# Two attention stages of a fused transformer kernel: heads normalised four at a time over DRAM, and row maxima seeded by their plain half

## The chip, the cores and the metric

The kernel runs on one core of one Trainium2 chip. The time is the device time of one execution in microseconds, the median of several runs. The names in the profile are PE for TensorE's matmuls, PEld for its weight loads, DVE for VectorE, ACT for ScalarE, POOL for GpSimd, and SP (SPq) for the queue of SyncE, which issues the DMAs spoken of here.

## The reference

Input x is 2 x 1024 tokens of 512 features in float32. Six blocks are added to it in turn, each on the layer norm of x:

```
x = x + 0.5 * ffn0(ln(x))          stage 0, f0: quantised, hidden 1536
x = x + attn0(ln(x))               stage 1, a0: 16 query heads, 4 kv heads, rope, biases
x = x + 0.5 * ffn0(ln(x))          stage 2, f0
x = x + 0.5 * ffn1(ln(x))          stage 3, f1: hidden 2048
x = x + attn1(ln(x))               stage 4, a1: 16 heads
x = x + 0.5 * ffn1(ln(x))          stage 5, f1

attention of one head, head size 32, 1024 tokens:
  att = q @ k.T / sqrt(32), causal mask, softmax over keys
  y   = att @ v ;  out = concat(heads) @ Wo
```

## The kernel before

One program, `make_plan`, writes a list of steps in order. Each engine walks that list and issues its own part of each step, so the list fixes the order on every engine and on the queue of SP. Semaphores carry the dependences. PSUM has eight banks, and `bank_turns` assigns them along the plan with a rough pace model (`Pace`).

An attention stage (stages 1 and 4) has two batches of 16 heads, 32 heads in all, in eight **groups** of four (numbered 0 to 7; `HPG` is 4). A head has eight **units** of 128 keys, a group has 32 units. Unit `u` of the main loop in `attention` issues, in this order: the side jobs that are due (`side.tick`), the row maxima of unit `u + 13` (`row_unit`, `AHEAD` is 13), the scores of the unit's keys against all later queries (`key`, L1148, whose exponential ScalarE takes at L1335), the diagonal mask and sum of two units on GpSimd (`e_mask` L1660, `e_add` L1671), and at odd units the products with v and with ones for two units nine back (`pv` L1167, `den` L1178). Beside the loop run side jobs: the projection of the next group (`piece`, L1094), layer norms, the output projection.

**Row maxima.** For a tile of 128 queries `row` (L1130) makes the scores against all earlier keys. Up to 512 keys are one piece, more are two equal halves (`row_pieces`). VectorE takes the minimum of the negated masked scores of each piece with `tensor_tensor_reduce` (L1501), which also writes into PSUM and is followed by a read of the accumulator. Second halves go to columns 8 to 11 of `negmax`, and `row_min` (L1510) joins them. The eight maxima are transposed (`m_tp`, L1137), split in two (`m_hi`, `m_lo`) and written by SP into two rows of the query stack (`m_lo`, L1755), which `key` waits for.

**Stacks.** Before the rows of a group can run, SP copies each head's projected q (in stage 4, and every fourth group of stage 1, k as well) into `qst` and `kst`, three DMAs each (`stack`, L1745). The four heads of the next group are stacked at units 18, 20, 26 and 31 (`STACKS_AT`). Since rows run 13 units ahead, the first row of the next group stands in unit 19.

**The end of a head.** `pv` and `den` leave in one bank 256 columns of sums and 256 columns of denominators, in four quarters of 32 partitions, the same denominator in all 32 partitions of a quarter. `y_fin` takes the reciprocal of 128x256 (L1540) and multiplies (L1544) into `ysb`, and frees the bank; `y_move` (L1764) brings the four quarters into the head's 32 partitions of `y`. After the fourth head of a group `y_hi` (ScalarE, L1343) and `y_lo` (VectorE, L1554) make `yT`, and eight output products (`oproj`) and additions (`x_sum`, L1568) follow, one a unit, at units 16 to 23 of the next group. `y` is one tile: `y_move` waits for `y_lo` of the group before.

```
for c in range(HPG):
    sp.dma_start(T[s]["y"][j * HD:(j + 1) * HD, c * QUAD:(c + 1) * QUAD],
                 T[s]["ysb"][n % 2][c * HD:(c + 1) * HD, :]).then_inc(moved[n % 2], 16)
```

Of the kernel before, what the change touches and what calls it, by code (L numbers as in the profile page):

```python
# [8 lines left out]
F32 = mybir.dt.float32  # L9
# [8 lines left out]
P = 128  # L18
# [36 lines left out]
YT_AT = 2  # L55
O_LAG = 1
# [27 lines left out]
def into_heads(s):  # L84
    return s + 1 < len(STAGES) and not is_ffn(s + 1)

# [50 lines left out]
def make_plan():  # L137
# [112 lines left out]
    def attention(s, left):  # L250
# [18 lines left out]
        def row_unit(u):  # L269
            n, i = divmod(u, ST)  # L270
            if n < HEADS_ALL:
# [3 lines left out]
                if i == ST - 1:  # L275
                    plan.append(("row_min", s, n))
# [45 lines left out]
        for g in range(GROUPS_ALL):  # L322
# [6 lines left out]
            put([split(s, "o", g, 0)], at + O_W_AT, 0)  # L329
# [18 lines left out]
        def times_v(n, jt):  # L348
# [5 lines left out]
            if k == PAIRS - 1:  # L354
                job = [[]] * Y_AT + [[("y_fin", s, n)]] + [[]] * Y_WAIT + [[("y_move", s, n)]]
                g, j = divmod(n, HPG)
                if j == HPG - 1:
                    job += [[]] * YT_AT + [[("y_hi", s, g)]] + [[("y_lo", s, g)]] + [[]] * O_LAG
                    job += timed(*((O_STEP * t, ("oproj", s, g, t)) for t in range(ST)),
                                 *((O_STEP * t + X_AFTER, ("x_sum", s, g, t)) for t in range(ST)))  # L360
                side.start(job)
# [63 lines left out]
    "row": ("s_q", "row_max"), "row_min": ("row_min",), "m_tp": ("m_tp",), "m_hi": ("m_hi",), "m_lo": ("m_lo",),  # L425
    "key": ("s_k", "exp"), "e_mask": ("e_mask",), "pv": ("pv",),
    "e_add": ("e_add",), "den": ("den",), "y_fin": ("y_rec", "y_fin"),
# [59 lines left out]
class Pace:  # L487
# [10 lines left out]
    def run(self, step, banks):  # L498
# [84 lines left out]
        elif kind == "y_fin":  # L583
            done[step] = work("dve", 0.9, ("pv", s, where[0], ST - 1))
        elif kind == "y_hi":
            done[step] = work("act", 1.1, ("y_fin", s, (where[0] + 1) * HPG - 1))
# [9 lines left out]
def bank_turns(plan):  # L596
# [5 lines left out]
    for step in plan:  # L602
        width = banks_wanted(step)
        needs = []
        if width:
# [13 lines left out]
            if step[0] == "pv":  # L619
                release["y_fin", step[1], step[2]] = mine  # L620
# [44 lines left out]
def build(nc, a, out):  # L665
# [6 lines left out]
    with ExitStack() as ctx:  # L672
# [17 lines left out]
        moved = [ctx.enter_context(nc.semaphore(f"moved{i}")) for i in range(2)]  # L690
        stored = ctx.enter_context(nc.semaphore("stored"))
# [26 lines left out]
        for s, kind in enumerate(STAGES):  # L718
            t = T[s] = {}
            with ExitStack() as sc:  # L720
# [47 lines left out]
                else:  # L768
# [12 lines left out]
                    t["negmax"] = [sbuf(sc, f"{tag}negmax{i}", [P, ST + CT]) for i in range(2)]  # L781
# [7 lines left out]
                    t["rden"] = [sbuf(sc, f"{tag}rden{i}", [P, QUAD]) for i in range(2)]  # L789
                    t["ysb"] = [sbuf(sc, f"{tag}ysb{i}", [P, QUAD]) for i in range(2)]  # L790

        def gave_way(s):
# [123 lines left out]

        def quarters_of(y):
# [931 lines left out]
```

## Time and profile before

| | |
|---|---|
| Runs | 2629.57, 2633.96, 2639.21 us, median 2633.96 |
| Span of the profiled execution | 2632.3 us (the profile gives no other time of its own for it; it lies between the runs) |
| PE busy, PEld busy | 2535.4 us (96%), 2013.0 us (76%) |
| DVE, ACT, POOL busy | 1533.2 (58%), 1035.6 (39%), 981.6 us (37%) |
| First attention stage, units of groups 0 to 7 | 344 to 763 us of the span |
| Second attention stage, the same | 1623 to 2076 us |
| DMA traffic | 128.73 MB, mean 49 GB/s |

Busy shares of the whole span mix stages with different limits. The two attention stages take a third of the time, and only they are touched. The two feed-forward kinds run matmul after matmul. In the attention stages all four compute engines and SP take part, and what sets the time must be read from who waits for whom there. Matmuls are pipelined and their ends are modelled, so a busy PE is not PE at its peak.

### The profile page before, as it was taken

To read this page: it belongs to the slowest core of one execution; us is meant where nothing else is said; L and a number is where in the kernel's file an instruction comes from. 1 tells how busy PE (TensorE), PEld (TensorE's weight loads), DVE (VectorE), ACT (ScalarE), POOL (GpSimd) and SP (SyncE) were. 2 spreads that over 40 slices of the span, in tenths; PEclk is the share of its full clock that TensorE was granted. 3 is DMA by queue.
4 is the path that set the end of the run, shared out by engine and by line. 5 is a ranking of instruction groups with operands and counts; after the bars stand their busy time and mean duration, and the time that the engine had idled before them with its cause. 6 is when DMAs were issued, how large, how long until landed. Compare 5 with 4: busy or idle time off the path is not lost.

```text
span 2632.3 us, 44135 instructions
## 1 busy us (share of the span) xinstructions
PE 2535.4 (96%) x16928; PEld 2013.0 (76%) x16928; DVE 1533.2 (58%) x3356; ACT 1035.6 (39%) x1885; POOL 981.6 (37%) x1373
## 2 busy tenths in 40 slices
PE   6999989999999999999999999999999999999999
PEld 4788867667668888888888878677776678888887
DVE  7777579979975445433333345798589643333333
ACT  6555346656653223311111133566466431111111
POOL 5333566666643225211111122666366521111110
PEclk9999989999999999999999999999999999999999
DMA  4222131222220110100000002343233100000001
GB/s 148 73 73 73 39 76 46 51 68 64 48 93 1 36 45 12 37 25 25 24 25 25 25 17 58 92 94 75 52 88 79 37 32 25 24 25 25 25 17 64
DMA packets 72002, 128.73 MB, mean 49 GB/s; under 512 B 15728, under 2 KB 24944, under 8 KB 71792
## 3 DMA queue, kind: packets, MB, share of 16 engines
q1 hardware_dynamic: 71792, 125.92, 17.3%
q8 instruction: 134, 2.20, 0.4%
q14 instruction: 76, 0.62, 0.1%
HBM read 62.42 MB, written 13.63 MB: 29 GB/s over the span
## 4 chain that ended last, share of the span: by engine, by line
PE 81%; DVE 6%; POOL 2%; ACT 2%; SPq 2%; issue 2%; DMA 1%; DVEq 0%; ACTq 0%; POOLq 0%
PE psum L1049 65%; PE psum L1167 5%; PE psum L1130 4%; PE psum L1148 4%; PE psum L1178 2%; DVE psum L1501 2%; SPq L1745 1%; PE psum L1058 1%; DVE s1a0rden L1540 1%; ACT s1a0e L1335 1%; SPq L1764 0%; POOL s1a0e L1671 0%; ACT s4a1e L1335 0%; PE psum L1137 0%; POOL rstd L1610 0%
## 5 line engine op out<-in xcount | busy, mean ns | idle before, releaser
L1501 DVE CUSTOM_DVE_ANT_0 psum<-psum,mask_q 128x512 f32<-128x512 f32 (+5 forms) x768 | 413.2, 574 | 101.2 <-PE psum L1130 97.3
L1049 PE MATMUL psum<-hA_hi,wmem 128*128 128x256 f32 (+1 forms) x1536 | 405.2, 334 | 0.5 <-DVE s1a0negmax L1501 0.3
L1049 PEld LDWEIGHTS psum<-hA_hi,wmem 128*128 128x128 f32 x1536 | 270.3, 190 | 31.8 <-DVE s1a0negmax L1501 1.5
L1049 PE MATMUL psum<-hA_lo,wmem 128*128 128x512 f32 (+1 forms) x864 | 293.8, 340 | 0.0
L1335 ACT ACTIVATE s4a1e<-psum,p_scale 128x384 f32<-128x384 f32 (+5 forms) x384 | 205.5, 581 | 95.2 <-PE psum L1148 91.8
L1335 ACT ACTIVATE s1a0e<-psum,p_scale 128x384 f32<-128x384 f32 (+5 forms) x384 | 202.4, 578 | 78.1 <-PE psum L1148 76.8
L1454 DVE SCALAR_TENSOR_TENSOR x<-psum,x 128x512 f32<-128x512 f32 x256 | 175.7, 689 | 97.4 <-PE psum L1049 93.9
L1425 DVE TENSOR_TENSOR s5f1prod<-psum,s5f1silu 128x512 f32<-128x512 f32 x64 | 44.2, 691 | 303.7 <-PE psum L1049 303.7
L1425 DVE TENSOR_TENSOR s3f1prod<-psum,s3f1silu 128x512 f32<-128x512 f32 x64 | 44.2, 691 | 294.2 <-PE psum L1049 294.2
L1635 POOL TENSOR_TENSOR wmem<-raw,wmem 128x512 fp32r<-128x512 f32 x58 | 74.3, 1290 | 315.7 <-ACT wmem L1237 315.7
L1049 PE MATMUL psum<-s3f1w,s3f1a 128*128 128x512 f32 x768 | 181.6, 390 | 0.9 <-POOL s3f1w L1635 0.9
L1049 PE MATMUL psum<-s5f1w,s5f1a 128*128 128x512 f32 x768 | 180.0, 390 | 1.6 <-POOL s5f1w L1635 1.6
L1049 PEld LDWEIGHTS psum<-hA_lo,wmem 128*128 128x128 f32 x864 | 164.8, 191 | 19.8
L1671 POOL TENSOR_TENSOR s4a1e<-s4a1e 128x896 f32<-128x896 f32 (+3 forms) x128 | 164.8, 1288 | 17.4 <-ACT s4a1e L1335 6.4
L1671 POOL TENSOR_TENSOR s1a0e<-s1a0e 128x896 f32<-128x896 f32 (+3 forms) x128 | 164.6, 1286 | 17.1 <-ACT s1a0e L1335 5.8
L1049 PEld LDWEIGHTS psum<-s5f1w,s5f1a 128*128 128x128 f32 x768 | 143.9, 188 | 32.3 <-issue 2.0
L1049 PEld LDWEIGHTS psum<-s3f1w,s3f1a 128*128 128x128 f32 x768 | 143.5, 188 | 31.1 <-DVE s3f1prod L1425 1.1
L1645 POOL TENSOR_TENSOR x<-x,s0f0dso 128x512 f32<-128x512 f32 x64 | 89.0, 1412 | 136.1 <-DVE s0f0dso L1449 136.1
L1660 POOL TENSOR_SCALAR_AFFINE_SELECT s4a1e<-s4a1e 128x128 f32<-128x128 f32 x256 | 74.9, 299 | 166.6 <-ACT s4a1e L1335 164.9
L1635 POOL TENSOR_TENSOR s5f1w<-raw,s5f1w 128x512 fp32r<-128x512 f32 x32 | 40.8, 1296 | 242.4 <-ACT s5f1w L1237 242.4
L1635 POOL TENSOR_TENSOR s3f1w<-raw,s3f1w 128x512 fp32r<-128x512 f32 x32 | 40.8, 1295 | 241.4 <-ACT s3f1w L1237 241.4
L1148 PE MATMUL psum<-s1a0qst,s1a0kst 98*128 98x384 f32 (+4 forms) x384 | 118.1, 362 | 12.9 <-ACT s1a0e L1335 7.8
(195 smaller groups left out, 5581.8 us busy)
## 6 DMA issues: line engine op xcount, KB each, us to landing
s1a0qst<-s1a0qs SPq DMA_DIRECT2D x96, 128.0 KB, 2.3
s4a1qst<-s4a1qs SPq DMA_DIRECT2D x96, 128.0 KB, 2.4
s4a1kst<-s4a1ks SPq DMA_DIRECT2D x96, 128.0 KB, 2.4
raw<-in_gate SPq DMA_DIRECT2D x44, 256.0 KB, 2.9
raw<-in_up SPq DMA_DIRECT2D x44, 256.0 KB, 2.8
raw<-in_down SPq DMA_DIRECT2D x44, 256.0 KB, 2.8
rounded<-s0f0w SPq DMA_DIRECT2D x24, 256.0 KB, 2.0
s2f0w<-rounded SPq DMA_DIRECT2D x24, 256.0 KB, 4.9
```

The costliest lines, as they stand in the source:

```text
L1049: ins = pe.matmul(out_, w, m, start=n == 0, stop=n == len(terms) - 1)
L1130: pe.matmul(ps[:, 0, 0:pw], q_st[0:STACK, j, i * P:(i + 1) * P], k_st[0:STACK, j, z * pw:(z + 1) * pw], start=True, stop=True).then_inc(se ...
L1148: pe.matmul(ps[:, 0, 0:pw], k_st[0:STACK + 2, j, jt * P:(jt + 1) * P], q_st[0:STACK + 2, j, q0 + z * pw:q0 + (z + 1) * pw], start=True, st ...
L1167: ins = pe.matmul(psum[c * HD:(c + 1) * HD, bank, jt * HD:QUAD], v[:, jt, kv, :], e[:, :, c, :], start=jt == 0, stop=jt == ST - 1, skip_gr ...
L1335: act.activation(T[s]["e32"][:, begin_ + z * pw:begin_ + (z + 1) * pw - skip], src, ACT.Exp, bias=p_scale[:]).then_inc(sem["exp"], 1)
L1425: dve.tensor_tensor(prod[:], psum[:, bank, :], silu[:], ALU.mult).then_inc(sem["prod"], 1)
L1454: dve.scalar_tensor_tensor(x[:, tile, :], src, 0.5, x[:, tile, :], ALU.mult, ALU.add).then_inc(sem["x_add"], 1)
L1501: dve.tensor_tensor_reduce(scores, scores, mask_q[:, first:first + pw], -1.0, -MASKED, ALU.add, ALU.min, T[s]["negmax"][n % 2][:, column:c ...
L1635: pool.tensor_tensor(lo, buf[:], hi.bitcast(F32), ALU.subtract).then_inc(sem["w_lo"], 1)
L1645: pool.tensor_tensor(x[:, tile, :], x[:, tile, :], T[s]["dso"][nth(*step) % 2][:], ALU.add).then_inc(sem["x_pool"], 1)
L1660: pool.affine_select(out=block, in_=block, compare_op=ALU.is_ge, fill=0.0, base=0, pattern=[[1, P]], channel_multiplier=-1).then_inc(sem[" ...
L1671: pool.tensor_tensor(e32[:, begin + P:end], e32[:, begin + P:end], e32[:, more:more_end], ALU.add).then_inc(sem["e_add"], 1)
```

## The change

For groups 0 to 6 of each stage (`in_place(g)` is true for group 7 alone) the end of a head goes another way:

- `y_out`: ScalarE copies the whole bank, 128x512, to `ysb` (now 512 columns wide), where the plan had `y_fin`.
- `y_save`: SP writes `ysb` to DRAM (`heads_out`, 256 KB). After the fourth head, `y_load` reads the sums of each head back into its 32 partitions of `y` (four DMAs of 128 KB a group), and `den_in` reads one denominator of each query into a compact tile of 128x32 (16 KB).
- `y_rec`: VectorE takes the reciprocal of that tile. `y_keep` writes it to DRAM (`rdens`), `y_spread` reads it back with each head's row repeated over its 32 partitions (128x1024, 512 KB) into `yT[HI]`, which is free then. `y_norm`: VectorE multiplies `y` by it, 128x1024.
- `y_hi`, `y_lo` and the output products follow, nine units later than before: `y_lo` stands at unit 23 and the products at units 25 to 32. The output weight of the next group is fetched after the products, not at unit 23.

Group 7 keeps `y_fin` and `y_move`. The plan places of one group are, counted in units of the group after it: `y_out` of its last head 7, `y_save` 9, last `y_load` and `den_in` 12, `y_rec` 14, `y_keep` 15, `y_spread` 17, `y_norm` 21, `y_hi` 22, `y_lo` 23.

Row maxima in two pieces: the first half, which has no masked element, is now a `tensor_reduce` with maximum and negation straight from PSUM; the second half's `tensor_tensor_reduce` takes that result as its initial value and waits for its semaphore. `row_min` and the four extra columns are gone. `Pace` gets new durations for these steps, which moves bank assignments.

```
-                plan.append(("row_min", s, n))
...
                 g, j = divmod(n, HPG)
+                if in_place(g):
+                    job = [[]] * Y_AT + [[("y_fin", s, n)]] + [[]] * Y_WAIT + [[("y_move", s, n)]]
+                    job += [[]] * YT_AT
+                else:
+                    job = [[]] * Y_AT + [[("y_out", s, n)]] + [[]] * SAVE_WAIT
+                    job += [[("y_load", s, m) for m in range(n - j, n) if j == HPG - 1]
+                            + [("y_save", s, n)]]
+                    job += [[]] * LOAD_WAIT
                 if j == HPG - 1:
+                    if not in_place(g):
+                        job += timed((0, ("y_load", s, n)), (0, ("den_in", s, g)),
+                                     (REC_AT, ("y_rec", s, g)), (KEEP_AT, ("y_keep", s, g)),
+                                     (SPREAD_AT, ("y_spread", s, g)), (NORM_AT, ("y_norm", s, g)))
+                    job += [[("y_hi", s, g)]] + [[("y_lo", s, g)]] + [[]] * O_LAG
...
+                negmax = T[s]["negmax"][n % 2][:, i:i + 1]
+                if z + 1 < row_pieces(i):
+                    dve.tensor_reduce(negmax, scores, AX.X, ALU.max,
+                                      negate=True).then_inc(sem["row_max"], 1)
+                    return
+                if z:
+                    on.wait_ge(sem["row_max"], at("row_max", "row", s, n, i, z - 1))
+                dve.tensor_tensor_reduce(scores, scores, mask_q[:, first:first + pw], -1.0,
+                                         negmax if z else -MASKED, ALU.add, ALU.min,
+                                         negmax).then_inc(sem["row_max"], 1)
...
+            def y_out(s, n):
+                if n >= 2:
+                    on.wait_ge(*ysb_left(s, n - 2))
+                on.wait_ge(sem["pv"], at("pv", "pv", s, n, ST - 1))
+                act.activation(T[s]["ysb"][n % 2][:], psum[:, banks["pv", s, n, 0][0], :],
+                               ACT.Copy).then_inc(sem["y_out"], 1)
...
+            def y_rec(s, g):
+                on.wait_ge(den_loaded, 16 * (nth("y_rec", s, g) + 1))
+                dve.reciprocal(T[s]["rden"][:], T[s]["den"][:]).then_inc(sem["y_rec"], 1)
+
+            def y_norm(s, g):
+                on.wait_ge(y_loaded, HPG * 16 * (nth("y_norm", s, g) + 1))
+                on.wait_ge(rden_spread, 16 * (nth("y_norm", s, g) + 1))
+                y = T[s]["y"]
+                dve.tensor_tensor(y[:], y[:], T[s]["spread"], ALU.mult).then_inc(sem["y_norm"], 1)
...
+            def y_keep(s, g):
+                k = nth("y_keep", s, g)
+                on.wait_ge(sem["y_rec"], at("y_rec", "y_rec", s, g))
...
+            def y_spread(s, g):
+                k = nth("y_spread", s, g)
+                on.wait_ge(rden_kept, 16 * (k + 1))
+                if g:
+                    on.wait_ge(sem["o_proj"], at("o_proj", "oproj", s, g - 1, ST - 1))
+                sp.dma_start(T[s]["spread"], rdens[k % 2].unsqueeze(1).broadcast_to([HPG, HD, SEQ])
+                             ).then_inc(rden_spread, 16)
```

How the instructions move, in three places. First VectorE in units 14 and 15 of group 5 in the first stage, before (`ISA` is the maximum and the accumulator read behind it, in turn):

```order
L1501 ISA psum,s1a0negmax<-psum,mask_q 128x448
L1501 ISA s1a0negmax 128x1
L1501 ISA psum,s1a0negmax<-psum,mask_q 128x448
L1501 ISA s1a0negmax 128x1
L1554 TENSOR_TENSOR s1a0yT<-s1a0y,s1a0yT 128x1024
L1501 ISA psum,s1a0negmax<-psum,mask_q 128x512
L1501 ISA s1a0negmax 128x1
L1501 ISA psum,s1a0negmax<-psum,mask_q 128x512
L1501 ISA s1a0negmax 128x1
L1540 RECIPROCAL s1a0rden<-psum 128x256
L1544 TENSOR_TENSOR s1a0ysb<-psum,s1a0rden 128x256
```

and in the changed kernel:

```order
L1563 TENSOR_REDUCE s1a0negmax<-psum 128x1
L1568 ISA psum,s1a0negmax<-psum,mask_q,s1a0negmax 128x448
L1568 ISA s1a0negmax 128x1
L1607 RECIPROCAL s1a0den<-s1a0den 128x32
L1563 TENSOR_REDUCE s1a0negmax<-psum 128x1
L1568 ISA psum,s1a0negmax<-psum,mask_q,s1a0negmax 128x512
L1568 ISA s1a0negmax 128x1
```

The plain half is one instruction in place of two. `y_rec` (the 128x32 reciprocal) stands between rows 6 and 7, where `y_lo` stood; the wide reciprocal and product of the head are gone.

Second the queue of SP in the same group, units 12 to 20, before (`s1a0mrow` is `m_lo`, `raw<-in_q` a weight, `s1a0qst<-s1a0qs` a stack, `s1a0y<-s1a0ysb` is `y_move`):

```order
L1764 DMA s1a0y<-s1a0ysb 32x256 x4
L1755 DMA s1a0qst<-s1a0mrow 1x8x128 x2
L1723 DMA raw<-in_q 128x512
L1745 DMA s1a0qst<-s1a0qs 32x1024 x3
L1764 DMA s1a0y<-s1a0ysb 32x256 x4
L1745 DMA s1a0qst<-s1a0qs 32x1024 x3
L1755 DMA s1a0qst<-s1a0mrow 1x8x128 x2
```

and in the changed kernel (`rdens<-s1a0den` is `y_keep`, `s1a0yT<-rdens` `y_spread`, `heads_out<-s1a0ysb` `y_save`):

```order
L1856 DMA s1a0den<-heads_out 128x1x32
L1821 DMA s1a0qst<-s1a0mrow 1x8x128 x2
L1864 DMA rdens<-s1a0den 128x32
L1789 DMA raw<-in_q 128x512
L1872 DMA s1a0yT<-rdens 128x1x1024
L1839 DMA heads_out<-s1a0ysb 128x512
L1811 DMA s1a0qst<-s1a0qs 32x1024 x6
L1821 DMA s1a0qst<-s1a0mrow 1x8x128 x2
```

`y_keep`, `y_spread` and the save of the next group's first head now stand ahead of the first stack; before, `y_move` of that head stood behind it.

Third SP at the end of group 7, from unit 12 on, before:

```order
L1745 DMA s1a0qst<-s1a0qs 32x1024 x3
L1734 DMA wmem<-rounded 128x512
L1764 DMA s1a0y<-s1a0ysb 32x256 x4
L1755 DMA s1a0qst<-s1a0mrow 1x8x128 x2
L1734 DMA wmem<-rounded 128x512 x2
L1764 DMA s1a0y<-s1a0ysb 32x256 x4
```

and in the changed kernel:

```order
L1821 DMA s1a0qst<-s1a0mrow 1x8x128 x2
L1800 DMA wmem<-rounded 128x512
L1864 DMA rdens<-s1a0den 128x32
L1872 DMA s1a0yT<-rdens 128x1x1024
L1800 DMA wmem<-rounded 128x512
L1830 DMA s1a0y<-s1a0ysb 32x256 x4
L1821 DMA s1a0qst<-s1a0mrow 1x8x128 x2
```

The first `y_move` of group 7 stands ahead of the last `m_lo` in both; the `y_lo` of group 6 for which it waits has moved on VectorE from unit 14 to unit 23.

## Rows read from the trace of the kernel before

**Rows 1.** Stretches: us, busy (x) of PE, PEld, DVE, ACT, POOL, clock, DMA share, GB/s

```profile
616.00:664.00 48.00, 46.85 (x544) 34.60 (x547) 45.09 (x128) 29.50 (x59) 32.73 (x50) 1.00 0.24 57
...
1020.00:1600.00 580.00, 576.68 (x2611) 475.31 (x2610) 215.93 (x346) 141.88 (x240) 108.08 (x131) 1.00 0.09 26
```

**Rows 2.** Who waited (us, times) for L1501, L1335 and L1745, in turn

```profile
  PEld psum L1130: 8.7, 21
...
  PE psum L1049: 0.3, 2
...
  PEld psum L1148: 30.7, 44
...
  PE psum L1130: 5.4, 9
...
  PE psum L1130: 8.3, 6
```

**Rows 3.** Groups of instructions by line: busy us, mean ns, idle before

```profile
L1540 DVE RECIPROCAL s1a0rden<-psum 128x256 f32<-128x256 f32 x32 | 55.9, 1745 | 6.4 <-PE psum L1167 6.4
...
L1544 DVE TENSOR_TENSOR s1a0ysb<-psum,s1a0rden 128x256 f32<-128x256 f32 x32 | 13.6, 424 | 2.2
...
L1510 DVE TENSOR_TENSOR s1a0negmax<-s1a0negmax 128x4 f32<-128x4 f32 x32 | 14.9, 465 | 1.1
...
L1554 DVE TENSOR_TENSOR s1a0yT<-s1a0y,s1a0yT 128x1024 fp32r<-128x1024 f32 x8 | 9.9, 1234 | 1.6 <-ACT s1a0yT L1343 1.6
...
L1343 ACT ACTIVATE s1a0yT<-s1a0y 128x1024 fp32r<-128x1024 f32 x7 | 7.4, 1057 | 2.1 <-DMA s1a0y<-s1a0ysb 2.1
...
L1501 DVE CUSTOM_DVE_ANT_0 psum<-psum,mask_q 128x512 f32<-128x512 f32 x82 | 55.8, 707 | 18.2 <-PE psum L1130 18.2
```

**Rows 4.** Timeline of DVE, group 5, stage 1: start us, us, what

```profile
639.52 0.13 DVE L1501 DVE_READ_ACCUMULATOR2_ANT s1a0negmax<- 128x1 f32 x1
```

**Rows 5.** Timeline of SP and PE, the same group

```profile
638.17 0.43 SPq L1723 DMA_DIRECT2D raw<-in_q  x1
638.70 1.82 SPq L1745 DMA_DIRECT2D s1a0qst<-s1a0qs  x3
...
639.80 0.63 PE L1148 MATMUL psum<-s1a0qst,s1a0kst 98*128 98x512 f32 x2
...
640.83 0.47 PE L1049 MATMUL psum<-s1a0ow,s1a0yT 128*128 128x512 f32 x1 [0.40 <-issue]
...
644.94 0.86 PE L1049 MATMUL psum<-s1a0ow,s1a0yT 128*128 128x512 f32 x3
645.64 0.40 PE L1130 MATMUL psum<-s1a0kst,s1a0qst 96*128 96x512 f32 x1
```

**Rows 6.** DMA issues: queue, op, count, KB each, median us to landing

```profile
s1a0qst<-s1a0qs SPq DMA_DIRECT2D x96, 128.0 KB, 2.3
...
rounded<-s0f0w SPq DMA_DIRECT2D x24, 256.0 KB, 2.0
```

**Rows 7.** Timeline of PE, group 5 of stage 4

```profile
1950.14 0.62 PE L1148 MATMUL psum<-s4a1qst,s4a1kst 98*128 98x512 f32 x2
...
1955.38 0.39 PE L1130 MATMUL psum<-s4a1kst,s4a1qst 96*128 96x512 f32 x1
```

**Rows 8.** Timelines of ACT, SP and PE at the end of stage 1

```profile
754.98 0.47 ACT L1335 ACTIVATE s1a0e<-psum,p_scale 128x256 f32<-128x256 f32 x1 [1.17 <-PE psum L1148]
...
748.06 2.48 SPq L1764 DMA_DIRECT2D s1a0y<-s1a0ysb  x4
...
752.48 1.38 SPq L1755 DMA_DIRECT2D s1a0qst<-s1a0mrow  x2
...
756.91 1.04 PE L1148 MATMUL psum<-s1a0qst,s1a0kst 98*128 98x512 f32 x4
```

**Rows 9.** Stretches around a wait for a stack; columns as in rows 1

```profile
534.00:537.00 3.00, 1.11 (x6) 0.62 (x4) 2.76 (x4) 1.54 (x4) 2.84 (x3) 1.00 0.61 132
537.00:541.00 4.00, 3.46 (x28) 2.08 (x29) 1.30 (x3) 0.95 (x2) 2.31 (x4) 0.57 0.33 76
```

More of the change, by code:

```diff
@@ L328, in attention @@
                 put(group_weights(s, g + 2), at + QK_W_AT, 2)
-            put([split(s, "o", g, 0)], at + O_W_AT, 0)
+            if g == 0:
+                put([split(s, "o", g, 0)], at + O_W_AT, 0)
             if g % HPG == 2:
@@ L424 @@
     "bias_x": ("x_pool",),
-    "row": ("s_q", "row_max"), "row_min": ("row_min",), "m_tp": ("m_tp",), "m_hi": ("m_hi",), "m_lo": ("m_lo",),
+    "row": ("s_q", "row_max"), "m_tp": ("m_tp",), "m_hi": ("m_hi",), "m_lo": ("m_lo",),
     "key": ("s_k", "exp"), "e_mask": ("e_mask",), "pv": ("pv",),
-    "e_add": ("e_add",), "den": ("den",), "y_fin": ("y_rec", "y_fin"),
+    "e_add": ("e_add",), "den": ("den",), "y_fin": ("y_den", "y_fin"), "y_out": ("y_out",),
+    "y_rec": ("y_rec",), "y_norm": ("y_norm",),
     "y_hi": ("y_hi",), "y_lo": ("y_lo",), "oproj": ("o_proj",), "x_sum": ("x_add",),
@@ L690, in build @@
         moved = [ctx.enter_context(nc.semaphore(f"moved{i}")) for i in range(2)]
+        saved = [ctx.enter_context(nc.semaphore(f"saved{i}")) for i in range(2)]
+        y_loaded = ctx.enter_context(nc.semaphore("y_loaded"))
+        den_loaded = ctx.enter_context(nc.semaphore("den_loaded"))
+        rden_kept = ctx.enter_context(nc.semaphore("rden_kept"))
+        rden_spread = ctx.enter_context(nc.semaphore("rden_spread"))
+        heads_out = nc.dram_tensor("heads_out", (2, HPG, P, CH), F32, kind="Internal").ap()
+        rdens = nc.dram_tensor("rdens", (2, HPG, SEQ), F32, kind="Internal").ap()
         stored = ctx.enter_context(nc.semaphore("stored"))
@@ L915, in y_moved, with y_saved, ysb_left, y_whole @@
             return moved[n % 2], HPG * 16 * (nth("y_move", s, n) // 2 + 1)
+        def y_saved(s, n):
+            return saved[n % 2], 16 * (nth("y_save", s, n) // 2 + 1)
+        def ysb_left(s, n):
+            return y_moved(s, n) if in_place(n // HPG) else y_saved(s, n)
+        def y_whole(s, g):
+            if in_place(g):
+                return [y_moved(s, n) for n in range((g + 1) * HPG - 2, (g + 1) * HPG)]
+            return [(sem["y_norm"], at("y_norm", "y_norm", s, g))]
         def quarters_of(y):
@@ L1572, in vector_program @@
                      "q8": q8_, "q_b": q_b, "gu": gu, "a_lo": a_lo, "down": down,
-                     "turned": turned, "row": row, "row_min": row_min, "m_lo": m_lo, "v_out": v_out,
-                     "y_fin": y_fin, "y_lo": y_lo, "x_sum": x_sum, "piece_lo": piece_lo}
+                     "turned": turned, "row": row, "m_lo": m_lo, "v_out": v_out,
+                     "y_fin": y_fin, "y_rec": y_rec, "y_norm": y_norm, "y_lo": y_lo, "x_sum": x_sum, "piece_lo": piece_lo}
             for kind, *where in plan:
@@ L1769, in sync_program @@
+            steps = {"begin": begin, "open": open_, "y_move": y_move, "y_save": y_save, "y_load": y_load, "den_in": den_in,
+                     "y_keep": y_keep, "y_spread": y_spread, "x_in": x_in_, "w_in": w_in, "w_keep": w_keep,
                      "w_back": w_back, "stack": stack, "m_lo": m_lo}
```

99 lines of the change are left out of this document (63 added, 36 removed).

## The prediction

> **What bounds the kernel now.** I read the stretches first, one line for each group of four heads. A group without layer-norm work takes 48.0 us in the first attention stage: VectorE is busy for 45.1 of them, 94%, and TensorE for 46.9, 98%, so both look full [rows 1]. The waits tell them apart [rows 2]. In the whole span TensorE (matmuls and weight loads together) waited 20.9 us for the row maxima of L1501, in eight rows of which the first and the last are shown. For the exponentials of ScalarE, L1335, it waited four times as long: six rows from 30.7 to 5.4 us, 86 us together. Nobody waited for the reciprocal L1540. So VectorE is nearly full and yet seldom what TensorE waits for: it runs a unit or two behind TensorE and catches up inside the group. That limits the gain from a lighter VectorE to about 21 us of direct waits, of which I take 20, and a share of the 86 us that can't be read off.
>
> **What VectorE is spared, per group of four heads.** Removed: four reciprocals of 1.745 us and four products of 0.424 us, 8.7 us, and four row_min of 0.465 us, 1.9 us [rows 3]. Added: one reciprocal of 128x32, an eighth of the elements of L1540, so 0.2 us plus a fixed part, 0.3 us; one 128x1024 product like L1554, 1.2 us [rows 3]. The 16 unmasked halves lose the accumulator read of 0.13 us [rows 4], 2.1 us, and each masked half now waits for the semaphore of its plain half and reads a seed. No row shows a PSUM tensor_reduce. The nearest is L1501 itself, 0.707 us at 512 columns [rows 3]. If the reduce takes as long, 2.1 us are saved less 16 waits of 0.05 to 0.1 us; I take 1 us, with ends of 0 and 3. Sum: 8.7 + 1.9 + 1 - 0.3 - 1.2 = 10 us of 45. The Trainium skill, "VectorE: DVE Perf Modes", Rules for kernel authors, speaks against this part: tensor_reduce on a hot path is called the slowest DVE op, better restructured. By that rule the spared time would be 9 us and not 10, which changes no bound here.
>
> **What goes to ScalarE.** Four copies of 128x512 from PSUM per group. ScalarE is busy for 29.5 of 48 us [rows 1], so there is room, but each copy stands just before the two widest exponentials of the next head. The split of the output weight, which stood at unit 24 and ahead of the same exponentials, moves to a lighter place, and the bank of a head's output is free sooner. I cost these together at 0, with -10 and +15 us as ends.
>
> **The stack behind the new waits, a moved step that costs.** This is what the sum turns on. SP is one queue in order. At unit 14 or 15 it now meets y_keep, which waits for y_rec; then y_spread, which waits until y_keep has landed in DRAM; then the save of the next group's first head; and only then, at unit 18, the stack of that same next group's first head. TensorE needs that stack in unit 19, because rows run 13 units ahead of keys. Before, the stack had only finished pieces ahead of it and went out early. In group 5 of the first stage its three DMAs are issued from 638.70, its row matmul runs at 645.64, nearly 7 us later [rows 5].
>
> Now the same place after the change. The last maximum of row 6 ends at 639.65 [rows 4], so y_rec ends near 639.9. y_keep goes out at 639.95 and lands after 2.0 us, the time of a write to DRAM [rows 6]: 641.95. y_spread and y_save take about 0.45 us each to issue, as the whole-tile load ahead of the stack does (0.43) [rows 5]: 642.9. The three stack DMAs are issued in 1.82 us [rows 5], the third starts at 644.1 and lands 2.3 us later [rows 6]: 646.4. When is it wanted? From the key of unit 16 (639.80) to the row of unit 19 (645.64) are 5.84 us [rows 5]. They hold three output tiles of 0.70 us (644.94 to 645.64) and a wait of 0.4 us in front of them (640.83); these tiles move to units 25 on. That leaves 3.3 us, so it is wanted at 643.1. **TensorE waits 3.3 to 3.4 us.** In the second stage k is stacked too. Unit 16's key is at 1950.14 and the row at 1955.38 [rows 7]; less three tiles, 1953.3. The units ahead of it hold twice the projections, so VectorE is earlier against TensorE there; I put y_rec at 1949.2. Then 2.0 for y_keep, 0.9 for two issues, 3.0 until the sixth stack DMA starts, 2.3 to land: 1957.5. Wait 4.2 us. There are six groups per stage with both a spread and a following stack: 6 x 3.4 + 6 x 4.2 = 46 us. Waits for stacks cost 8.3 us now [rows 2] and are in that number already: **+38 us**. Ends: +15 if the chain is 2 us shorter than I think each time; +60 if the 512 KB spread and the 256 KB save, which stand in the DMA queue right ahead of the stack, hold up its landing by 1.5 us more.
>
> The Trainium skill, "DMA: Bandwidth & Descriptors", section "Latency and other measured facts", gives 0.8 us as the shortest round trip to DRAM, for tiny transfers such as this one of 16 KB. By that figure y_keep would cost 1.2 us less each time and the sum 14 us less. No row here shows so small a write, and the 2.0 us of the trace stand.
>
> **The last group.** It is normalised in place, and its first y_move waits for y_lo of group 6, since both use the one y tile. y_lo moves from unit 14 to unit 23; y_move stays at unit 18. SP stands still, and behind it is m_lo of head 31, which the key of unit 24 needs. Timed on the first stage [rows 8]: the exponential of unit 22 ends at 755.45, y_hi adds 1.06, y_lo 1.22 [rows 3], four y_move 2.48, the second m_lo starts 0.7 later and lands after 2.0 at most: 762.9. The key now starts at 756.91, and two output tiles ahead of it are gone. Wait 6 to 7.4 us per stage: **+14 us**, ends 6 and 20.
>
> **The clock.** From 534 to 537 TensorE was busy for 1.1 us only, since it waited for a stack; in most of the next 4 us the granted clock was at its lower level, 1.2 GHz [rows 9]. A mean of 0.57 over 4 us loses 1.7 us. I have 14 waits of 3.3 us or more and take it for five: **+8 us**, ends 0 and 24.
>
> **The sum.** 2632.3 (span) - 20 + 0 + 38 + 14 + 8 = 2672. The span of the profiled execution is 1.7 us under the median of the three runs (2634.0), so I take 2672 as the time too: 1.4% slower. A measurement of this kernel can tell about 0.3%, 8 us.
>
> **Rivals.**
> - *VectorE sets the pace (faster).* For: 94% busy against 72% for weight loads in the same line, 34.6 of 48 us, while the long feed-forward stretch reaches 82%, 475 of 580 us [rows 1]. By the Trainium skill, "Perfetto Trace Analysis", Identifying the Most-Contended Engine, matmul busy time doesn't count and the engine of highest occupancy is the one to relieve, which would be VectorE. Worked from the rows: the direct 21 us and a third of the 86 us go, 50 us, while SP's chain turns out shorter (+15) and the last group costs 10: 2607. Half of the 86 us and no stall at all would be 2568. Against: who waits for whom. Chance 0.18.
> - *It cancels.* The relief of the rival above with the stalls I forecast, less the clock: -50 + 38 + 14 = +2, 2634. Chance 0.10.
> - *The stalls as forecast, and the clock drops at nearly each of them, with transfers colliding:* -20 + 60 + 14 + 22 = +76, 2708. Chance 0.2, a part of slower.
> - *The maxima change nothing* (reduce, semaphore and seed eat the accumulator read and row_min): VectorE is still 7 us lighter per group; the time moves by under 5 us within the cases above.
>
> **How the numbers follow.** Slower, as forecast or worse: 0.52 + 0.2 = 0.72. Within 0.3%: 0.10. Faster: 0.18. The range leaves out the better half of the fast rival and what lies beyond the clock case: 2608 to 2712. Within the slower cases it is 2645 to 2712.
>
> **What would show it.** Right: in groups 1 to 6 TensorE waits for a DMA on the stacks at its row matmul (L1130 before), 3 us or more each, and group 5 of the first stage takes 49 us or more although VectorE's busy time in it falls to some 35 us; on SP the first stack of a group is issued after, not before, unit 17; near the end of both stages one wait of 6 us for the DMA of mrow; clock rows at 0.5 behind such waits. A reciprocal of about 0.3 us and a norm of 1.2 us. Wrong: groups of 45 us or less, stacks that land in time, or y_rec much earlier against TensorE than I timed it. If waits for the exponentials of ScalarE fall by more than a third, my bound on the gain was wrong.

## The result and the profile after

The changed kernel takes 2822.01 us (median of 4 runs, 2819.5 to 2827.24) against 2636.59 us before in the same session: a ratio of 1.071, 95% interval 1.0689 to 1.0732. The forecast was 2672, 1.4% slower; it is 7.1% slower, and the range ended at 2712.

The page of the changed kernel (line numbers are now the changed kernel's: rows L1184, keys L1202, stack L1811, y_keep L1864, y_spread L1872, y_save L1839):

```profile
span 2820.2 us, 43813 instructions
...
PE 2578.7 (91%) x16928; PEld 2042.8 (72%) x16928; DVE 1430.7 (51%) x2952; ACT 1060.1 (38%) x1941; POOL 990.3 (35%) x1373
...
PEclk9999998998989999999999999988988899999999
```

The span grew by 187.9 us. VectorE's busy time fell by 102 us; the forecast's 10 us in each of 14 groups would have made it 140. TensorE fell from 96 to 91% busy. The view of waits says what TensorE stood for (us in total, times, longest):

```profile
PE psum L1184 <- DMA s4a1kst<-s4a1ks: 78.9, 7, 14.0
PE psum L1184 <- DMA s1a0qst<-s1a0qs: 53.5, 5, 12.0
...
PE psum L1202 <- DMA s1a0qst<-s1a0mrow: 14.0, 4, 11.1
PE psum L1184 <- DMA s1a0kst<-s1a0ks: 13.9, 2, 11.7
...
PE psum L1202 <- DMA s4a1qst<-s4a1mrow: 10.1, 3, 8.1
```

The three rows on L1184 are the waits for stacks, 146.3 us in 14 waits, against 8.3 us before [rows 2]. Two of the 14 are short and have no spread in front of them: 2.1 us at the start of the first stage (2.1 before as well) and 3.3 us in group 0 of the second. The other twelve stand one in each of groups 1 to 6 of both stages, as forecast: 10.0 to 12.0 us each in the first stage and 11.9 to 14.0 in the second, 140.9 us together, where the forecast had 3.4 and 4.2. The two rows on L1202 hold the wait for m_lo at the end of each stage, 11.1 and 8.1 us, also where the forecast put it. One of the waits for a stack, in group 1 of the first stage, in the timelines of SP and then of PE:

```profile
412.35 0.35 SPq L1864 DMA_DIRECT2D rdens<-s1a0den  x1
412.74 0.44 SPq L1789 DMA_DIRECT2D raw<-in_q  x1
413.80 0.59 SPq L1872 DMA_DIRECT2D s1a0yT<-rdens  x1
414.45 0.46 SPq L1839 DMA_DIRECT2D heads_out<-s1a0ysb  x1
415.02 3.76 SPq L1811 DMA_DIRECT2D s1a0qst<-s1a0qs  x6
```

```profile
414.47 0.51 PE L1202 MATMUL psum<-s1a0qst,s1a0kst 98*128 98x384 f32 x2
425.32 0.77 PE L1184 MATMUL psum<-s1a0kst,s1a0qst 96*128 96x512 f32 x1 [10.35 <-DMA s1a0qst<-s1a0qs]
```

On SP all goes as forecast: y_keep to the start of the stack's third DMA takes 3.9 us (the forecast had 4.1). Then the chain of waits shows what was not forecast: 8.91 us from that issue to its landing, where the forecast put 2.3.

```profile
415.64 0.59 SPq L1811
416.23 0.04 issue
416.27 8.91 DMA s1a0qst<-s1a0qs
```

The same time in stretches (columns as in rows 1):

```profile
413.00:417.00 4.00, 1.97 (x27) 1.00 (x19) 2.07 (x8) 2.70 (x6) 2.95 (x4) 1.00 0.66 184
417.00:421.00 4.00, 0.00 (x0) 0.00 (x0) 0.00 (x0) 0.24 (x1) 1.00 (x2) 0.57 0.85 181
421.00:425.00 4.00, 0.00 (x0) 0.00 (x0) 0.00 (x0) 0.00 (x0) 0.00 (x0) 0.50 0.25 94
425.00:429.00 4.00, 3.68 (x30) 2.30 (x31) 0.76 (x2) 0.95 (x3) 1.81 (x2) 0.50 0.01 5
660.51:725.06 64.55, 50.85 (x559) 36.88 (x558) 38.59 (x104) 31.34 (x63) 33.35 (x51) 0.87 0.26 67
```

The last row is group 5 of the first stage: 64.6 us, where it took 48.5 by the same cut (first key of one group to first key of the next), with VectorE busy for 38.6 of them.

The groups by that cut (group 7 to the last key of its stage), which the experiments are read against, in us:

| kernel | stage 1, groups 0 to 7 | stage 4, groups 0 to 7 |
|---|---|---|
| before | 48.0 48.5 56.7 61.2 58.1 48.5 56.8 41.5 | 50.3 53.8 60.3 56.7 77.2 53.0 59.0 43.1 |
| after | 42.5 60.3 69.8 70.1 72.3 64.5 69.5 51.2 | 49.9 67.2 75.6 70.9 92.3 71.1 74.4 56.4 |

Group 0 has no spread in it, and it became shorter, by 5.5 us in the first stage and 0.4 in the second. Every other one became 9 to 18 us longer.

### The profile page after: what moved, and what is told of

Read it like the earlier page. It is cut to its first block, busy times and chain, and to the rows that moved or that the text cites. A ratio compares the mean times of both kernels' runs of the same rounds, so it can differ in the third digit from the quotient of the medians.

```text
span 2820.2 us, 43813 instructions
## 1 busy us (share of the span) xinstructions
PE 2578.7 (91%) x16928; PEld 2042.8 (72%) x16928; DVE 1430.7 (51%) x2952; ACT 1060.1 (38%) x1941; POOL 990.3 (35%) x1373
## 4 chain that ended last, share of the span: by engine, by line
PE 77%; DMA 7%; DVE 6%; SPq 2%; issue 2%; ACT 2%; POOL 1%; DVEq 0%; ACTq 0%; POOLq 0%
PE psum L1103 62%; PE psum L1221 5%; PE psum L1184 4%; PE psum L1202 4%; DMA s4a1kst<-s4a1ks 2%; PE psum L1232 2%; DMA s1a0qst<-s1a0qs 2%; SPq L1811 1%; DVE psum L1568 1%; PE psum L1112 1%; DVE s1a0negmax L1563 1%; DVE s4a1negmax L1563 1%; DMA s1a0kst<-s1a0ks 0%; DMA rdens<-s4a1den 0%; PE psum L1191 0%
## 5 line engine op out<-in xcount | busy, mean ns | idle before, releaser
L1568 DVE CUSTOM_DVE_ANT_0 psum<-psum,mask_q 128x512 f32<-128x512 f32 (+3 forms) x256 | 125.4, 503 | 252.3 <-PE psum L1184 250.9
L1184 PE MATMUL psum<-s4a1kst,s4a1qst 96*128 96x512 f32 (+4 forms) x384 | 127.9, 392 | 80.6 <-DMA s4a1kst<-s4a1ks 78.9
L1486 DVE TENSOR_TENSOR s5f1prod<-psum,s5f1silu 128x512 f32<-128x512 f32 x64 | 44.3, 692 | 303.5 <-PE psum L1103 303.5
L1486 DVE TENSOR_TENSOR s3f1prod<-psum,s3f1silu 128x512 f32<-128x512 f32 x64 | 44.3, 692 | 294.1 <-PE psum L1103 294.1
L1184 PE MATMUL psum<-s1a0kst,s1a0qst 96*128 96x512 f32 (+4 forms) x384 | 127.1, 391 | 68.8 <-DMA s1a0qst<-s1a0qs 53.5
L1184 PEld LDWEIGHTS psum<-s4a1kst,s4a1qst 96*128 96x128 f32 x384 | 69.5, 200 | 103.4 <-issue 87.0
L1202 PE MATMUL psum<-s1a0qst,s1a0kst 98*128 98x384 f32 (+4 forms) x384 | 122.8, 372 | 22.7 <-DMA s1a0qst<-s1a0mrow 14.0
```

The costliest lines, as they stand in the source:

```text
L1184: pe.matmul(ps[:, 0, 0:pw], q_st[0:STACK, j, i * P:(i + 1) * P], k_st[0:STACK, j, z * pw:(z + 1) * pw], start=True, stop=True).then_inc(se ...
L1202: pe.matmul(ps[:, 0, 0:pw], k_st[0:STACK + 2, j, jt * P:(jt + 1) * P], q_st[0:STACK + 2, j, q0 + z * pw:q0 + (z + 1) * pw], start=True, st ...
L1486: dve.tensor_tensor(prod[:], psum[:, bank, :], silu[:], ALU.mult).then_inc(sem["prod"], 1)
L1568: dve.tensor_tensor_reduce(scores, scores, mask_q[:, first:first + pw], -1.0, negmax if z else -MASKED, ALU.add, ALU.min, negmax).then_inc ...
```

## The experiments

Three questions: what made the stacks land 9 us late; what the parts cost one by one; and what the idea could bring with all waits mended. The kernel before was timed beside every experiment, at a median of 2635.96 to 2638.67 us.

### The spread's transfer: same rows, or four heads outermost

`y_spread` is one DMA that reads four rows of 4 KB, each 32 times, as [4 heads, 32, 1024]. Theory S: the cut over the DMA engines goes by that outermost 4. Theory H: 128 reads of the same few rows hinder each other. First, other rows, same shape:

```
-sp.dma_start(T[s]["spread"], rdens[k % 2].unsqueeze(1).broadcast_to([HPG, HD, SEQ]))
+rows = heads_out[g % 2].rearrange("j (a b) q -> j a (b q)", b=2)[:, 0:HD, :]
+sp.dma_start(T[s]["spread"], rows)
```

> The changed kernel with y_spread reading 128 different rows of 4 KB (from heads_out, 4 heads x 32 rows) in place of each head's one row 32 times over; outermost dimension 4 as in the change. The normalisation then multiplies by other numbers: the spread of the reciprocals is left out, its transfer's size and shape are kept. Theory S: nothing changes, 2822 within 12, waits for stacks of 10 us each. Theory H: the transfer takes 3 us, waits of 2 to 5 us, 2690.

Measured: 2833.35 us, 1.0734 of before (1.0712 to 1.0756), against 1.071 for the change. The waits for stacks are 86.8, 60.2 and 15.9 us, 163 together. Reading 128 different rows is no faster, 11 us slower if anything: H falls, and the time lies within theory S's 12 us.

Then the same rows in another shape, one transfer for each head:

```
+for j in range(HPG):
+    sp.dma_start(T[s]["spread"][j * HD:(j + 1) * HD, :],
+                 rdens[k % 2, j].unsqueeze(0).broadcast_to([HD, SEQ]))
```

> The changed kernel with y_spread as four transfers, one for each head: 32 rows of 4 KB from that head's one row of DRAM, so that the outermost dimension of each is 32 and not 4; same place on SP, three more issues of 0.45 us ahead of the stack. Theory S (the one transfer of the change is cut along its outermost dimension of 4, so four of the sixteen DMA engines carry all of it and the stack's pieces queue behind it there): the four transfers use all sixteen, the spread is through in 2 to 3 us, and TensorE's 14 waits for stacks fall from 10.4 us each (146 us together) to 4 to 5 (the 3.4 of SP's queue and 1.3 for the issues), 65 us together; time 2715 (2695 to 2745). Theory Q (it is SP's order alone that makes the stack late): waits as before or longer, 2820 or more.

Measured: 2743.17 us, 1.0391 (1.0365 to 1.0416): 79 us less than the change, with the same 512 KB in four issues. Waits of TensorE, and the stretches that answer to those above:

```profile
PE psum L1184 <- DMA s4a1kst<-s4a1ks: 39.0, 7, 7.0
PE psum L1184 <- DMA s1a0qst<-s1a0qs: 29.6, 6, 5.8
```

```profile
415.50:419.50 4.00, 1.99 (x27) 0.99 (x19) 2.07 (x8) 2.65 (x6) 2.95 (x4) 1.00 0.66 196
419.50:423.50 4.00, 0.44 (x1) 0.47 (x2) 0.00 (x0) 0.30 (x1) 1.01 (x2) 0.79 0.96 246
423.50:427.50 4.00, 4.00 (x32) 2.50 (x32) 1.25 (x3) 1.21 (x3) 1.83 (x2) 0.50 0.11 24
```

The stretch at a share of 0.25 is gone: 0.96, then done. The waits are 75.1 us in 15 (with 6.5 in 2 for k). The twelve behind a spread take 67.3 of them, 5.3 us each in the first stage and 5.9 in the second. The forecast's 3.4 and 4.2 with three more issues of 0.45 would be 4.8 and 5.6. Together the two runs show that the way the transfer was cut made the landing late, not the rows read. The four transfers differ from the one in two things, the outermost dimension and the size of each; one transfer with the 32 rows outermost (`spread_turned`) gave no result, so these two aren't separated. That four engines carried it is read from the share of 0.25; which engine a packet ran on the profile doesn't show. The Trainium skill has this as a rule, "DMA: Bandwidth & Descriptors", Rules for kernel authors: an outermost dimension of fewer than 16, a leading zero-stride broadcast for example, confines the whole transfer to at most that many engines. Both runs agree with it: a share of 0.25 with 4 outermost, 0.96 with 32.

### The order on SP

Here the transfer stays as it is, and what waits moves behind the stacks; the edit of `tail_later` below is in it, with 12 units and not 6.

```
-REC_AT, KEEP_AT, SPREAD_AT, NORM_AT = 2, 3, 5, 9
+REC_AT, KEEP_AT, SPREAD_AT, NORM_AT = 2, 7, 9, 15
```

> The changed kernel with y_spread's transfer as it is (outermost dimension 4) but y_keep, y_spread and y_norm 4 to 6 units later, behind the first two stacks on SP, and the first y_move of the last group behind m_lo of head 31 (alone worth 16.5 us: 2805.5). The stacks have 7 units from issue to use where they stood 1. Theory: both, a late issue and the slow transfer ahead, hurt only because the stack is behind them; here the waits for stacks fall under 20 us together, the clock comes back, and the time is 2625 (2605 to 2650), whatever the spread takes. Rival: DMA engines are what is short: m_lo and the other stacks meet the spread instead, waits move to L1202 and to y_norm, 2680 or more.

Measured: 2753.27 us, 1.0426 (1.04 to 1.0452): 52 us less than `tail_later`, not 180. The time is the rival's, and so is half of its mechanism. The waits for stacks fell to 33 us (24.2, 4.7, 4.4) and those for m_lo are 5.8 us, but the slow transfer is now late for `y_norm`, on VectorE, and TensorE's row matmul waits for VectorE's row maxima:

```profile
DVE s4a1y L1615 <- DMA s4a1yT<-rdens: 32.0, 7, 7.6
...
DVE s1a0y L1615 <- DMA s1a0yT<-rdens: 20.7, 6, 6.0
...
PE psum L1186 <- DVE s4a1negmax L1565: 15.4, 5, 5.9
...
PE psum L1186 <- DVE s1a0negmax L1565: 12.2, 6, 2.8
```

VectorE stood for it 52.7 us with the row maxima queued behind. The slow transfer costs in both places that were tried. Both mended, `y_spread` as four transfers and `NORM_AT` 13:

> As order_tail, with y_spread as four transfers over all engines, and y_norm two units earlier. If the place in the queue is all that matters, within 8 us of order_tail. If the four loaded DMA engines still delay something (m_lo, later stacks), 10 to 30 us faster than order_tail. Against the kernel before: VectorE has 7 us less per group from the normalisation and 1.6 us more from the maxima; if VectorE sets the pace in the groups, 2570 to 2600; if TensorE does, 2610 to 2630.

Measured: 2697.67 us, 1.0224 (1.019 to 1.0258), 56 us less than with the slow transfer, more than the 10 to 30 expected if four loaded engines still delayed something (`y_norm` moved too). Still 60 us over before. The next section has its twin with the old maxima; SP's timeline there showed what was left in front of the stack:

```profile
1996.88 0.34 SPq L1844 DMA_DIRECT2D heads_out<-s4a1ysb  x1
1997.33 1.82 SPq L1816 DMA_DIRECT2D s4a1qst<-s4a1qs  x3
1999.19 1.85 SPq L1816 DMA_DIRECT2D s4a1kst<-s4a1ks  x3
```

The stack is issued 0.45 us after y_save (the row on heads_out), which waits for ScalarE's copy y_out; it starts 33.6 us after the start of its group. In the kernel before it started at 1947.22, 26.0 us after, and 2.9 before the key of unit 16 [rows 7]:

```profile
1947.22 2.63 SPq L1745 DMA_DIRECT2D s4a1qst<-s4a1qs  x3
```

The last groups were longer too, 47.6 and 49.4 us against 41.5 and 43.1. So y_save of a group's first head went behind the stack as well, and the delay by four units was dropped for group 6, which has no stack behind it:

```
+by = LATER if g + 2 < GROUPS_ALL else 0          # LATER = 4
-job = [[]] * Y_AT + [[("y_out", s, n)]] + [[]] * SAVE_WAIT
+job = [[]] * Y_AT + [[("y_out", s, n)]] + [[]] * (SAVE_WAIT + (2 if j == 0 else 0))
```

> The changed kernel with y_spread as four transfers, the first y_move of the last group behind m_lo of head 31, and SP's order mended wholly: y_keep, y_spread and y_norm four units later (but not in the group ahead of the last, which has no stack behind it), and the save of a group's first head behind the first stack and no longer ahead of it. Theory: in four_order_tail the stack still stood behind y_save, which waits for ScalarE's copy y_out (a stack issued at 1997.33, 0.45 behind the save), and the last groups lost 5 us each and 11 us at the end of the first stage to output tiles pushed behind the last head. With both mended the waits for stacks go back to the 8 us of the kernel before, and the time falls from 2698 to 2640 (2620 to 2660). Rival: ScalarE's copies and the larger traffic hold the time, 2675 or more.

Measured: 2661.12 us, 1.0083 (1.0065 to 1.0101), 1 us above the theory's range; waits for k stacks 11.8 and 4.7 us. The mean clock was 0.992 in the profiled execution, the fastest of six (2649.70), and 0.984 to 0.988 in the others; before it was 0.988 to 0.994. So the spread's shape, the places on SP and what followed from them (the clock among it) account for about 160 of the 185 us.

### The end of a stage

```
+wait = Y_WAIT + (MOVE_LATER if j == 0 else 0)     # MOVE_LATER = 6
-job = [[]] * Y_AT + [[("y_fin", s, n)]] + [[]] * Y_WAIT + [[("y_move", s, n)]]
+job = [[]] * Y_AT + [[("y_fin", s, n)]] + [[]] * wait + [[("y_move", s, n)]]
```

> The changed kernel with the first y_move of a head group that is normalised in place (head 28) six units later, behind m_lo of head 31. Theory: the waits of TensorE for m_lo at the end of the two stages, 11.1 and 8.1 us, were SP standing at that y_move for y_lo of group 6; they go, the last groups take 9 and 11 us less with the clock, 2802 (2795 to 2808). Rival: head 30's y_fin or the exponentials take the wait's place, under 8 us gained, 2814 or more.

Measured: 2805.53 us, 1.0637 (1.0621 to 1.0653): 16.5 us less than the change. Group 7 takes 45.8 and 44.3 us (51.2 and 56.4). In the first stage half of the wait is still there, 5.6 us of 11.1. The slow spread fits it: y_spread of group 6 was issued at 818.80 and m_lo of head 31 from 823.03, and from 826 to 830, with TensorE idle, the DMA share was 0.35. In `save_after_stack`, with four transfers, the waits for m_lo are 4.7 us in all. The forecast term was 14, and its mechanism holds.

### The maxima

The kernel before with the change's maxima alone (its diff is the part on `row` and `row_min` of the change):

> The kernel before with the maxima of the change alone: plain tensor_reduce on unmasked halves, their result as the masked half's initial value, no row_min; reciprocals and products as before. By the profile of the change a plain reduce of 512 columns takes 0.68 us where the old operation with its accumulator read took 0.85; the masked half with a seed takes 0.06 more, and some 0.15 us stand between the two. So the pair costs the same and only row_min goes, 0.47 to 0.65 us x 64 = 35 us of VectorE. TensorE waits for the row maxima 21 us in all: expected -6 us, 2630 (2620 to 2637). Rival A (it is the new pair that costs: the masked half stands still behind the plain one): 2645 or more. Rival B (VectorE sets the pace): -25 us or more, 2610.

Measured: 2654.77 us, 1.0068 (1.0053 to 1.0083). This half of the change costs 18 us on its own: rival A. The reason stands in VectorE's timeline. Before, a pair of halves of 448 columns:

```profile
638.35 0.65 DVE L1501 CUSTOM_DVE_ANT_0 psum<-psum,mask_q 128x448 f32<-128x448 f32 x1
638.94 0.13 DVE L1501 DVE_READ_ACCUMULATOR2_ANT s1a0negmax<- 128x1 f32 x1
638.94 0.66 DVE L1501 CUSTOM_DVE_ANT_0 psum<-psum,mask_q 128x448 f32<-128x448 f32 x1
...
639.52 1.21 DVE L1554 TENSOR_TENSOR s1a0yT<-s1a0y,s1a0yT 128x1024 fp32r<-128x1024 f32 x1
```

And in `maxima_alone`:

```profile
648.52 0.62 DVE L1504 TENSOR_REDUCE s1a0negmax<-psum 128x1 f32<-128x448 f32 x1
649.29 0.69 DVE L1509 CUSTOM_DVE_ANT_0 psum<-psum,mask_q,s1a0negmax 128x448 f32<-128x448 f32 x1
649.90 0.14 DVE L1509 DVE_READ_ACCUMULATOR2_ANT s1a0negmax<- 128x1 f32 x1
```

Read the starts, not the durations. Before, the accumulator read starts at the same time as the next operation, and both overlap the end of the one ahead: two halves in 638.35 to 639.52, 1.17 us. Now the masked half waits for its plain half to be wholly done: 0.77 from start to start, and the pair takes 1.38 (to 649.90). That is 0.21 us more for each of 16 pairs, 3.4 us a group, against four row_min, 1.9 [rows 3]. Net 1.5 us. By the cut above the groups of the first stage grew by 2.0 us each and those of the second, where row_min takes 0.647 us a head and not 0.465, by 1.1, 24.8 us together. (The profiled execution here took 2659.45 us, 5 over the median, so these numbers run high.) The accumulator read that the change saves had cost nothing.

The normalisation alone, with the old maxima:

> The changed kernel with the maxima of the kernel before (both halves masked, then row_min): the normalisation half of the change alone. If the maxima cost their 18 us here too, as on the kernel before, 2804. If VectorE has slack in a kernel that stands still for stacks, as in the pair with and without them at 2698 and 2699, 2822 within 6 and the whole loss is the normalisation's.

Measured: 2801.12 us, 1.062 (1.0603 to 1.0637), 21 us less than the change. My expectation that idle time would swallow the maxima fell. Its waits for stacks are 138.2 us (74.8, 50.2, 13.2) against 146.3: y_rec stands behind seven such pairs on VectorE, so faster pairs send y_keep off sooner: against the key of unit 16 it went out up to 0.8 us earlier. That is 8 of the 28.6 us between the two profiled executions (this one was 8 us under its median). TensorE's busy time is 15.1 us shorter (2563.6 against 2578.7) at a mean clock of 0.960 against 0.955; how much of that is the clock isn't settled. In the mended kernels the two maxima differ by 1 us and by 5, no more than their runs scatter:

> As four_order_tail with the maxima of the kernel before (both halves masked, row_min). The maxima alone cost 18 us on the kernel before, where VectorE was nearly full: start to start a pair of halves of 448 columns took 1.17 us and takes 1.38, since the reduce can't overlap the masked half that waits for it. If VectorE still sets the pace here: 15 to 20 us faster than four_order_tail. If VectorE has slack now, within 6 us of it. Time 2595 (2570 to 2620).

Measured: 2698.89 us, 1.0223 (1.0197 to 1.025), against 2697.67. The 2595 was missed by 104 us: VectorE wasn't what held this kernel.

> As save_after_stack with the maxima of the kernel before. With the waits gone, VectorE should matter again: 10 to 15 us faster than save_after_stack, 2628 (2605 to 2645), about the kernel before or a little faster. If VectorE has slack since the normalisation left it 7 us a group, within 6 us of save_after_stack. Faster than the kernel before by over 8 us only if the lighter VectorE is worth something in the clean groups: 48.5 us in group 5 of the first stage would be 47 or less.

Measured: 2655.72 us, 1.0069 (1.0056 to 1.0083), against 2661.12: inside the rival's 6 us. It is the best version of the idea and still 0.7% slower than before. Its groups:

| stage | groups 0 to 7, us |
|---|---|
| 1 | 45.0 45.9 59.6 62.0 57.7 49.9 57.3 48.3 |
| 4 | 45.8 53.9 62.2 59.4 80.1 58.0 61.9 47.0 |

Groups 0 gain 3.0 and 4.5 us; the largest losses are in the last groups, 6.8 and 3.9, and in group 5 of stage 4, 5.0. By the view of waits, matmuls and weight loads together, TensorE stood 43 us for the exponentials where it stood 94 before, and 53 us for row maxima and row_min where it stood 23. So the route over DRAM does shorten the wait for ScalarE, and another wait takes the gain.

### What is the idea worth?

Group 7 was to be mended by taking group 6 in place too (`in_place(g)` true from 6 on):

> As save_after_stack_oldmax (2656), with the last two groups of a stage normalised in place and not the last alone; six of eight groups go over DRAM. Theory: what is left of the loss there stands mainly in the last groups, 48.3 and 47.0 us against 41.5 and 43.1, because the output tiles of group 6 come 8 units later by the way over DRAM and TensorE has nothing to put in their place; in place they come back, -11 us, and group 6 of the second stage loses its wait for the stack, -2: 2643 (2635 to 2650). Rival: VectorE, with the reciprocals of two groups again, gives it back, or the first y_move of group 6 now holds m_lo: 2652 or more.

Measured: 2671.85 us, 1.0131 (1.011 to 1.0152): worse by 16 us, the time of the rival. The first stage's groups 6 and 7 take 62.6 and 54.1 us, longer still. The theory that the late output tiles were the cause is not borne out, and the cause of the long last groups stays open. The edit changed the moves and VectorE's load there along with them, and the first `y_move` of group 7 went back to its early place.

Last, the ceiling. On the kernel before, ScalarE copies the undivided sums and VectorE does nothing at the end of a head:

```
-dve.reciprocal(rden[:], psum[:, bank, QUAD:CH]).then_inc(sem["y_rec"], 1)
-dve.tensor_tensor(T[s]["ysb"][n % 2][:], psum[:, bank, 0:QUAD], rden[:], ALU.mult)
+act.activation(T[s]["ysb"][n % 2][:], psum[:, banks["pv", s, n, 0][0], 0:QUAD], ACT.Copy)
```

> The kernel before with the division left out: ScalarE copies each head's 256 columns of numerators where VectorE took the reciprocal and the product; nothing is divided by the sums of exponentials, everything else, the moves by SP too, is as before. It is what the idea could give at the very best: VectorE is 8.5 us lighter per group (2.12 start to start, four times) and nothing goes over DRAM. Theory T (TensorE is the bound of the groups, 98% busy): -15 to -35 us, 2615 (2600 to 2623), most of it in the groups where TensorE was idle (0, 3 and 4). Theory V (VectorE sets the pace, as the +2.0 us per group for +1.6 us of VectorE in maxima_alone suggests): the groups shrink until TensorE is full, 3 us and more in each of 16, 2585 or less.

Measured: 2630.21 us against 2635.96, 0.9975 (0.9966 to 0.9984). VectorE's busy time falls from 1533.2 to 1431.1 us, 6.4 a group, with nothing added but a ScalarE copy. (The two instructions taken out had held 139.0 us; row_min, which is unchanged, now shows 1.02 and 0.94 us in place of 0.47 and 0.65.) 6 us are gained, less than theory T's 15. The stretch of rows 1 in this kernel:

```profile
616.00:664.00 48.00, 46.98 (x556) 34.85 (x555) 40.43 (x121) 30.58 (x64) 32.66 (x50) 1.00 0.23 57
```

VectorE went from 45.1 to 40.4 us and TensorE from 46.9 to 47.0 [rows 1]; group 5 by the cut above went from 48.5 to 48.3. So VectorE isn't the bound, and with this plan a way of normalising that takes everything off VectorE for a ScalarE copy has 0.25% to win. That TensorE is the bound fits its 98% busy; no run made TensorE lighter to show it. The two engines are close: 1.5 us a group more on VectorE cost 18 us, and 6.4 less gained 6.

## Why the prediction was right or wrong

- **Direction and places: right.** TensorE waits for the stack at its row matmul in the groups named, and once at the end of each stage for m_lo; group 5 takes over 49 us with VectorE lighter (38.6 us, though, not 35); the clock is at 0.50 behind such waits.
- **The step that failed** is a price in the stack's term: "the third starts at 644.1 and lands 2.3 us later". Twelve waits of 3.4 and 4.2 us gave +38; the same twelve took 10.9 and 12.6 us, and the term is +138 (146.3 less 8.3). SP's chain was sized right (3.9 us against 4.1), and `spread_four`'s 5.3 and 5.9 us bear it out. The landing took 8.9 us in the wait shown, behind a y_spread that by the DMA share ran on a quarter of the DMA engines; cut in four it is gone. I priced y_spread by its issue of 0.45 us, and its transfer only in the upper end, by 1.5 us for 512 KB through all engines; I never asked how the transfer is cut up. The page of the Trainium skill that I cited for y_keep, "DMA: Bandwidth & Descriptors", has the rule, in Rules for kernel authors.
- **The last group: right.** 14 forecast; 16.5 by `tail_later`, 11.1 and 8.1 us of waits against 6 to 7.4.
- **The maxima: wrong sign.** "I take 1 us, with ends of 0 and 3" saved per group: it costs 3.4 per group, 1.5 after row_min, and 18 to 21 us in all, in the kernel before and in the change. I took 0.13 us per accumulator read off a sum of durations, when the read overlapped the next operation, and 0.05 to 0.1 us, a price that no row showed, for a wait that also ends that overlap and costs 0.21 us a pair of 448 columns. The rows to see it were there: the read of [rows 4] starts at 639.52, as the product behind it does.
- **The relief: too large,** 20 against the 6 of `undivided`. The bound of 21 us from direct waits was no gain to take whole: in `undivided` the same count of waits for L1501 still gives 18.2 us of 20.9, although VectorE is lighter. The rival in which VectorE sets the pace (2607) falls. The sign against my bound, waits for the exponentials down by more than a third, did come, 48 us in the changed kernel and 91 in `undivided` where 94 stood before. But no run turned it into time: the route over DRAM that shortens them brought waits for stacks, and mended, for row maxima.
- **The clock: too small,** 8 forecast with 24 as the end. For the same 16928 matmuls TensorE was busy 2578.7 us in place of 2535.4, 43 us more, at a mean clock of 0.955 against 0.992. In `norm_alone`, with the old maxima, it is 28 us more at 0.960; in `maxima_alone`, at 0.989, 21 us more, so the 43 us hold some of the maxima's cost too, and the clock's own share lies nearer 28. The rest of the 187.9 us is idle time of TensorE, 144.6: 138 for the stacks and 20.5 for m_lo (24.1 less the 3.6 before), less 14 for shorter waits, nearly all of them matmuls' waits for exponentials (11.6 us against 25.9).
- **y_save** ahead of the stack I priced by its issue; it also waits for ScalarE. Behind y_keep and y_spread that didn't show; with those moved, it, the delay of group 6's steps and the place of group 7's first y_move (12 units later, then 6) held 37 us together (2697.67 to 2661.12), and no run separates them.

## What to carry to other kernels

Before a DMA is put ahead of one that is needed soon, look at its outermost dimension on both sides as well as at its size: with 512 KB in the shape [4, 32, 1024] ahead of its stack TensorE stood 11.7 us each time, with four transfers of [32, 1024] at the same place 5.6. Price an operation by the distance from its start to the next start, never by its duration, and a wait on the operation just ahead by the overlap that it ends too. And before rebuilding a step to relieve an engine, leave the step out in one run: here that run would have said that there were 6 us to win.

## What the runs showed of the hardware

- y_spread with 4 outermost: a DMA share of 0.25 for 4 us, stacks landing up to 13.4 us after issue (median 2.6); as four transfers with 32 outermost a share of 0.96 and stacks landing after 4.3 us at most. Reading 4 rows 32 times or 128 different rows made no difference that helps (2822 and 2833 us).
- Behind each of the long waits the granted clock was at its lower level, 1.2 GHz: 0.50 from 421 to 429 us, with TensorE idle in the first half and 92% busy in the second.
- The accumulator read of 0.13 to 0.14 us adds nothing from start to start; VectorE's next operation starts with it, 0.06 to 0.08 us before the one ahead ends. A wait for VectorE's own last result costs some 0.15 us after that end: 0.77 us from start to start for 448 columns, where 0.59 were needed.
- A tensor_reduce of 512 PSUM columns took 0.68 us, the masked operation 0.70, with a seed 0.76. The Trainium skill, "VectorE: DVE Perf Modes", Rules for kernel authors, calls tensor_reduce on a hot path the slowest DVE op; the trace doesn't bear that out against the masked operation. Here it is the wait around it that costs.
- Landing of y_keep (16 KB in 128 rows to DRAM) took 1.4 us in the median, where the forecast took 2.0.
